# Adding the routed rows of a mixture of experts to the output by accumulating DRAM-to-DRAM transfers in place of loads and additions on DVE

## The reference

```
x = x + attention(layernorm(x))                 # linear attention, 16 heads of 8
x = x + cross_attention(ctx, layernorm(x))      # exponential feature maps, softmax over 77 keys
x = x + ffn(layernorm(x))
```

```
logits = hidden @ router_w.T                     # 16 experts
top_vals, top_idx = top_k(logits, 1)             # each token goes to one expert
routed = (up * silu(gate)) @ down_proj[expert]   # of hidden * sigmoid(top_val)
shared = (silu(hidden @ sg.T) * (hidden @ su.T)) @ sd.T   # width 512, for all tokens
x + shared + routed
```

## Time and profile before

| | us |
|---|---|
| median of 3 runs | 497.67 |
| lowest, highest | 497.08, 499.48 |
| the profiled execution | 495.24 |
| its span, first to last instruction | 493.4 |
| mean granted TensorE clock, share of full speed | 0.961 |
| PE / PEld busy | 412.9 / 309.3 |
| DVE / ACT / POOL busy | 298.1 / 264.1 / 201.1 |

### The profile page before, as it was taken

The page is one execution under the profiler, slowest core; times in us unless marked ns, Lnnn a source line. Parts: engine busy times, 40 slices in busy tenths (PEclk is TensorE's granted clock), DMA queues, the critical chain, the costliest instruction groups (busy, mean ns, idle before and its releaser), DMA issues.

```text
span 493.4 us, 10895 instructions
## 1 busy us (share of the span) xinstructions
PE 412.9 (84%) x3796; PEld 309.3 (63%) x3797; DVE 298.1 (60%) x881; ACT 264.1 (54%) x602; POOL 201.1 (41%) x280
## 2 busy tenths in 40 slices
PE   1788888876767738898999999999999997988995
PEld 1466666653444327788888888776656666677663
DVE  4787776541666665778787877365773333444446
ACT  5455555435878533777777777755563222333320
POOL 1322222111787554454555300000047753766740
PEclk9999999987998877999999999999999998999999
DMA  6940000000499994675766300000005115887729
GB/s 197 307 120 1 0 0 0 2 0 14 145 261 272 286 306 130 179 197 155 199 165 185 86 7 5 4 3 0 1 25 181 55 54 135 244 248 236 232 59 314
DMA packets 46449, 61.81 MB, mean 125 GB/s; under 512 B 7268, under 2 KB 42372, under 8 KB 44788
## 3 DMA queue, kind: packets, MB, share of 16 engines
q1 hardware_dynamic: 34800, 37.63, 25.7%
q0 software_dynamic: 4832, 20.37, 14.7%
q10 hardware_dynamic: 6768, 3.18, 2.6%
HBM read 43.34 MB, written 20.59 MB: 130 GB/s over the span
## 4 chain that ended last, share of the span: by engine, by line
PE 57%; DVE 18%; ACT 10%; issue 7%; SPq 3%; DMA 3%; ACTq 1%; DVEq 0%; POOL 0%
PE bank L709 6%; PE bank L698 5%; PE bank L1323 4%; PE bank L1268 3%; PE bank L1278 3%; PE bank L1277 3%; PE bank L671 3%; DVE mx L783 3%; ACT t_hT L1205 2%; PE bank L410 2%; PE bank L1324 2%; PE bank L733 2%; DMA kparts<-kpart 2%; PE bank L434 2%; PE bank L397 2%
## 5 line engine op out<-in xcount | busy, mean ns | idle before, releaser
L874 ACT ACTIVATE prob<-bank 77x512 f32<-77x512 f32 x128 | 74.4, 596 | 21.3 <-PE bank L698 21.1
L783 DVE TENSOR_REDUCE mx<-bank 128x5 f32<-128x385 f32 (+1 forms) x96 | 54.9, 576 | 17.1 <-PE bank L671 14.2
L1249 POOL DMA_INDIRECT sorted_in<-h_rows,pos_s x32 | 31.6, 986 | 80.4 <-ACT h_rows L1182 71.9
L1254 POOL DMA_INDIRECT routed<-t_y,t_no x47 | 45.4, 967 | 27.8 <-DVE t_y L1122 19.0
L698 PE MATMUL bank<-qst,kst 99*77 99x128 bf16 x512 | 50.2, 221 | 0.2 <-ACT prob L874 0.2
L377 POOL TENSOR_TENSOR qkv<-qkv,rn 128x256 f32<-128x256 f32 x32 | 19.1, 631 | 63.4 <-DVE rn L296 63.4
L1178 ACT ACTIVATE s_g<-bank 128x512 f32<-128x512 f32 x32 | 19.1, 598 | 47.3 <-PE bank L1278 33.7
L698 PEld LDWEIGHTS bank<-qst,kst 99*77 99x77 bf16 x512 | 38.5, 116 | 7.4 <-ACT prob L874 4.1
L671 PE MATMUL bank<-kst,qst 96*128 96x77 bf16 x512 | 35.6, 206 | 7.7 <-DVE mx L783 4.1
L1032 DVE TENSOR_TENSOR act<-bank,s_g 128x512 f32<-128x512 f32 x24 | 16.5, 688 | 34.9 <-ACT s_g L1178 34.9
L633 POOL DMA_DIRECT2D qst<-qparts x36 | 18.2, 505 | 47.3 <-DMA kst<-kparts 33.7
(11 more groups left out here) (169 smaller groups left out, 1018.6 us busy)
## 6 DMA issues: line engine op xcount, KB each, us to landing
qst<-qparts POOLq DMA_DIRECT2D x36, 256.0 KB, 3.5
t_w<-in_expert_w SPq DMA_DIRECT2D x47, 192.0 KB, 2.5
qparts<-qpart SPq DMA_DIRECT2D x16, 384.0 KB, 7.7
kst<-kparts POOLq DMA_DIRECT2D x36, 154.0 KB, 3.9
kparts<-kpart SPq DMA_DIRECT2D x16, 231.0 KB, 7.5
sorted_in<-in_fill SPq DMA_DIRECT2D x1, 3102.0 KB, 13.4
t_row<-sorted_in ACTq DMA_DIRECT2D x47, 66.0 KB, 1.9
qst<-qparts SPq DMA_DIRECT2D x12, 256.0 KB, 6.7
```

Source lines behind the costliest of these rows:

```text
L783: v.tensor_reduce(mx[:, b % JA, h0:h1], bank[n % 2][:, 0:(h1 - h0) * KEYS].rearrange("p (h k) -> p h k", k=KEYS), AX.X, ALU.max, negate=Tr ...
L874: a.activation(prob[n % PROBS][:].rearrange("p c t -> p (c t)"), bank[2 + n % 2][0:KEYS], ACT.Exp, scale=SCORE_SCALE).then_inc(s["expd"], 1)
L1249: p.indirect_dma_start(out=sorted_in, out_offset=bass.IndirectOffsetOnAxis(ap=pos[:, b:b + 1].bitcast(U32), axis=0), in_=h_rows[:, b], in_ ...
L1254: p.indirect_dma_start(out=routed, out_offset=bass.IndirectOffsetOnAxis(ap=t_no[r][:].bitcast(U32), axis=0), in_=t_y[r][:], in_offset=None ...
```

## The change

- The additions `add_routed` on DVE, the buffers `y_back` and their four loads are gone, and the semaphore `res_add` is no longer used.
- `store(g)` waits for `x3` (the shared expert's addition) in place of `res_add`, so it stores x + shared without the routed rows. Each store has a semaphore of its own, `stored[g]`. Stores 0 to 5 are issued by SP between the first ring of weight loads and the rest of them; stores 6 and 7 behind the last ring.
- Behind its last scatter POOL waits until all scatters have landed, and then for each group until `stored[g]` has come, and issues a transfer from `routed` to `out`, both in DRAM, that adds to what is there (`accum_op=ALU.add`): 512 rows of 512 bytes taken as 32 rows of 8 KB, 256 KB in all. POOL, and no longer SP, waits for the end (`res_out`).
- Tokens are numbered b * 128 + p, in the order of the output, so that group g is one contiguous piece of `routed`.

```diff
-        y_in = [sem(f"y_in{i}") for i in range(NG // 2)]
+        stored = [sem(f"stored{g}") for g in range(NG)]
...
-        y_back = [sb4(f"y_back{i}", [P, 2 * JP, D]) for i in range(NG // 2)]
...
-            def add_routed(g):
-                if g % 2 == 0:
-                    v.wait_ge(y_in[g // 2], 16)
-                v.wait_ge(s["x3"], max(g + 1, AHEAD_OF_TILES))
-                v.tensor_tensor(xs[:, g * JP:(g + 1) * JP], xs[:, g * JP:(g + 1) * JP], seqs(y_back[g // 2], g % 2), ALU.add).then_inc(s["res_add"], 1)
-
...
             behind_gated(5)
-            add_routed(0)
-            add_routed(1)
             behind_gated(6)
-            add_routed(2)
-            add_routed(3)
             behind_gated(7)
-            add_routed(4)
-            add_routed(5)
             behind_add(7)
-            add_routed(6)
-            add_routed(7)
...
             loop_tiles(body)
+            for r in range(RING):
+                p.wait_ge(t_out[r], len(range(r, TILES, RING)) * 16)
+            for g in range(NG):
+                p.wait_ge(stored[g], 16)
+                p.dma_start(out[g * JP:(g + 1) * JP].rearrange("b (a e) f -> (b a) (e f)", e=16),
+                            routed[g * GT:(g + 1) * GT].rearrange("(a e) f -> a (e f)", e=16), accum_op=ALU.add, max_dma_last_dim=4096).then_inc(s["res_out"], 16)
+            p.wait_ge(s["res_out"], NG * 16)
...
             load_ring(0, False)
+            for g in range(AHEAD_OF_TILES):
+                store(sp, g)
             for k in range(1, -(-TILES // RING)):
                 load_ring(k * RING, True)
-            for r in range(RING):
-                sp.wait_ge(t_out[r], len(range(r, TILES, RING)) * 16)
-            for g in range(NG):
-                if g % 2 == 0:
-                    sp.dma_start(y_back[g // 2][:], routed[0:TOK].rearrange("(p b) f -> p b f", p=P)[:, g * JP:(g + 2) * JP]).then_inc(y_in[g // 2], 16)
-            for g in range(NG):
+            for g in range(AHEAD_OF_TILES, NG):
                 store(sp, g)
-            sp.wait_ge(s["res_out"], NG * 16)
 
         def store(sp, g):
-            sp.wait_ge(s["res_add"], g + 1)
-            sp.dma_start(out[g * JP:(g + 1) * JP].rearrange("b p f -> p b f"), xs[:, g * JP:(g + 1) * JP]).then_inc(s["res_out"], 16)
+            sp.wait_ge(s["x3"], g + 1)
+            sp.dma_start(out[g * JP:(g + 1) * JP].rearrange("b p f -> p b f"), xs[:, g * JP:(g + 1) * JP]).then_inc(stored[g], 16)
...
-    second += [(r[:, None] * B + np.arange(B)[None, :]).astype(np.int32).view(f32)]
+    second += [(np.arange(B)[None, :] * P + r[:, None]).astype(np.int32).view(f32)]
```

## The result

The changed kernel takes 511.28 us in the median of 4 runs (510.36 to 511.70), against 497.38 (4 runs) for the kernel before: a ratio of 1.0267, 95% interval 1.0237 to 1.0297. It is slower by 13.9 us; I had forecast 4.2. The profiled execution took 510.88 and its span is 509.1, against 495.24 and 493.4.

A forecast was written before the change was run, and what follows sets the result against it. TensorE was taken to bound everything up to 488.95, with 4.45 us following. Store landing 491.76 + accumulation 4.4 + queueing 1.0 + closing 0.44 = 497.6 against 493.4, +4.2, so 501.9 us; range 498.7 to 512.0.

The forecast's parts named there:

- The end up to the last addition: Everything until behind_add(7) ends at 488.95 is TensorE's; the change leaves it as it was.
- The saving of 1.20: At the end on DVE: without the last two add_routed, the last store goes at 488.98 in place of 490.18.
- Early stores, pushed-back register loads, numbering at nothing: Stores 0 to 5 between weight loads, ring 1's value_load starting later, and the new token order: each priced at 0.
- The series of store and accumulation: At the end, group 7's accumulation can't begin until its store has landed: two transfers in series where one stood.
- The store at 2.78: Store 7, issued at 488.98, lands 2.78 later, at 491.76.
- the 14.4 us of work: On the transfer engines from 479.2: seven accumulations of 1.8 and two stores of 0.9, free at 493.6.
- The accumulation at 4.4, plus 1.0 of queueing: Group 7's accumulation takes 3.5 plus 0.9 for reading the destination, and waits 1.0 for the engines.
- The last wait moving from SP to POOL: At the program's end: POOL in place of SP waits for the last transfer, priced at 0 by itself.
- third rival: POOL's closing drain comes onto the path at the end: +5.6 or +10.5; chance 0.13.
- Rival 2: The accumulations are slow and pile up, so their queue sets the end: +7.4, +16 or +21; chance 0.22.
- Rival 3's second form: POOL's closing drain starts only once the last transfer has landed, 497.2 + 6.7 = 503.9: +10.5; chance 0.13 for both forms.
- Rival 4: Not slower: the seven earlier accumulations finish in time and the last lands within 3.7, under +2.5; chance 0.17.

The follow-up runs named there:

- run 8: Changed kernel with stores 0 to 5 moved back behind all weight loads: 560.48 us, ratio to before 1.0236.
- run 12: Changed kernel with the token numbers of before (p * 32 + b): 510.31 us in one execution, tail 17.3.
- run 3: Changed kernel with the accumulations of groups 0 to 6 left out, group 7's kept: 508.62 us, ratio to before 1.0184.
- run 7: Small separate kernel timing 256 KB DRAM to DRAM transfers: plain 2.8 us, accumulating 3.9; SP's store 2.3 alone, 7.2 or 7.4 behind six accumulations.
- run 13: Small separate kernel: SP's store behind six POOL transfers, 5.9 us plain, 7.2 or 6.7 accumulating; drains after 8 to 64 transfers, 0.082 us each plus 0.04.
- run 1: Kernel before, with POOL also waiting for the last store: 506.48 us against 499.58, ratio 1.0151.
- run 5: Changed kernel with an added POOL drain near its program's start, before any transfer: 555.44 us against 546.03, ratio 1.0145.
- run 6: Small separate kernel of POOL drains: 0.17 and 0.18 us after nothing, 0.12 after one transfer, 2.67 after 32 plain transfers or scatters.
- run 2: Changed kernel with SP, not POOL, waiting for the last accumulation: 505.98 us, ratio to before 1.0132.
- run 4: Changed kernel with an added POOL drain ahead of its wait for store 7: 502.95 us in one execution, tail 12.3.
- run 9: Changed kernel with an added POOL drain behind the scatters to sorted_in, ahead of the tiles: 506.23 us, ratio to before 1.0197.
- run 10: Changed kernel with groups 6 and 7 added on DVE as before, POOL accumulating only 0 to 5: 500.56 us against 497.71, ratio 1.0072.

## Why the prediction was wrong

The direction was right, the size was not: +4.2 forecast, +13.9 measured. That 511.28 lies inside the range (to 512.0) is owed to the room that I had given to the rivals, and is no merit of the sum. By its steps:

- **The end up to the last addition**: nothing moved. Right. `add_routed` had held nothing up; the last store goes 0.02 behind `behind_add(7)` (491.45). The saving of 1.20 is there.
- **Early stores, pushed-back register loads, numbering at nothing**: right (runs 8, 12). From the first to the last `t_hT` copy the tile stage takes 61.3 us, against 61.9 before.
- **The series of store and accumulation**: right as a mechanism. POOL's eighth transfer is issued 0.28 behind the landing of store 7.
- **The store at 2.78**: wrong, 5.57. I let group 7's accumulation queue behind the others (+1.0) but not its store, which goes through the same engines before it. My own sum contradicts itself here: it had both stores among the 14.4 us of work that kept the engines busy to 493.6, and yet store 7 landed at 491.76. The price of that queue was about right: from the first issue at 481.55 to the seventh's landing at 496.4 are 14.9 us. Store 6, forecast to land near 482.6, came at 487.0 for the same reason, and POOL's seventh transfer waited for it. In runs 3, 7 and 13 as well a store lands alone in 2.0 to 2.3, and otherwise just behind the transfers issued ahead of it. That is +2.8.
- **The accumulation at 4.4, plus 1.0 of queueing**: it took 4.0, and there was no queue left when it was issued. That is -1.4. The second read was priced at 0.9 and measured 1.1 (3.9 less 2.8); the engines' time for each at 1.8, measured 1.44. The rule of the Trainium skill that I had cited (Collectives: The Full Stack, "The bandwidth ceiling: the fold count and why AG ≠ RS ≠ AR", two source reads halve the rate) is borne out in kind: 1.44 against 0.86 is a factor of 1.7. The Trainium skill's 2.0 us plus bytes over 436 GB/s (DMA: Bandwidth & Descriptors, "Anatomy of one DMA — SWDGE (gpsimd) path") gave an estimate of 2.6: the plain copy took 2.8, the accumulation 3.9.
- **The last wait moving from SP to POOL "0 by itself"**: this is the step that failed. POOL's drain of 7.34 us comes behind its last wait. With what surrounds it, the span ends 7.8 after the last landing and not 0.44, +7.3. I had seen the row and made it my third rival, at 0.13, with the argument that nothing would be outstanding by then. Runs 1, 5, 6 and 13 show that this argument is wrong: the drain's work doesn't need a transfer in flight. It is left by transfers long landed. Run 2 shows the price of the wait on POOL by itself: with SP holding it, the tail is 3.3 shorter, and run 4 shows the rest, with a closing drain of 0.13.

Together: 4.2 + 2.8 + 0.3 (POOL's wake behind the landing) - 1.4 + 7.3 = 13.2, the growth of the tail.

Rival 2, accumulations that pile up, was right in a form I hadn't written: they did pile up, seven of them until 496.4, but what it cost was the store. Rival 3's second form (the drain starts once the transfer has landed, +10.5) was the mechanism; it too left the store at 2.78. Rival 4, not slower, would have failed without the drain as well: the tail would then be about 10, still 6 over before.

**Open.** With a single drain at the end of the full kernels, it is shorter than the count gives: 6.7 for 151 transfers and 7.34 for 159. The difference of eight fits (0.65), the sum doesn't (12.4 and 13.1). Yet both drains of run 9 fit, 8.6 for 104 and 4.54 for 55. So the number of transfers since the last drain is not the whole rule in a long program, and what shortens the single drain no run shows. In runs 4 and 10 the drain met transfers in flight and took 10.5 and 11.7. And why a store takes its place behind all that POOL issued before it, where both queues run on the same engines, was not taken further.

## What to carry to other kernels

Look at which engine holds the last wait, and at the closing rows behind the chain: POOL paid for the transfers that it had issued when its program ended, 0.082 us each in the small kernels and 7.34 for 159 in the changed one, and it is hidden only if POOL finishes early. SP's drain took 0.13 at most, so let SP wait for the end, or drain POOL where it is idle anyway. A transfer that needs another's landing is a series; price the first one too in the queue that it meets: here it landed just behind what was issued ahead of it. Additions on an engine that idled were cheaper than the same additions made by transfers: the eight on DVE cost 1.2 us at the end, and without them the kernel was 13.9 us slower.

## What the runs showed of the hardware that I had not expected

- In small kernels POOL's DRAIN takes 0.082 us for each transfer that POOL has issued since the last one: 0.69 for 8, 2.65 for 32, 5.26 for 64, though all had landed. In the full kernels it took 6.7 to 7.3 for 151 to 159. SP's takes 0.01 to 0.13.
- A semaphore wait doesn't work this off: POOL waited 9.2 us for store 7 and still drained for 7.34 (the changed kernel).
- A 256 KB store of SP lands in 2.0 to 2.3 alone, and in 5.9 to 7.4 behind six transfers of POOL, for plain and accumulating ones, their pieces 4 KB or 512 bytes, its own 512 bytes or 2 KB.
- DRAM to DRAM, 256 KB: 2.8 plain, 3.9 accumulating; in a row 0.86 and 1.44 for each further one.
